# A graph and expert kernel: edge index loads moved from the sync queue to GpSimd in an earlier stage, and two matmul operands stacked as bfloat16 parts

## The reference

```python
# layer 1: label encoder and two graph attention layers
x = jnp.concatenate([features, emb[input_labels]], axis=-1)
x = x @ le_W1.T + le_b1                      # 512 -> 1024
x = layernorm(x) * ln_g + ln_b; x = relu(x)
h = x @ le_W2.T + le_b2                      # then two _gat_layer(...)
# layer 2: 8 experts, each token goes to one
hmid = relu(einsum('ecd,edf->ecf', buf, w1) + b1[:, None, :])
ybuf = einsum('ecf,efd->ecd', hmid, w2) + b2[:, None, :]
# layer 3: gated graph layer
Wh = x @ W_w + W_b; Uh = x @ U_w + U_b; Vh = x @ V_w + V_b
sigma = sigmoid((Wh * attn_l)[src] + (Wh * attn_r)[dst])
h = Uh + segment_sum(Vh[src] * sigma, dst) / (segment_sum(sigma, dst) + 1e-06)
# layer 4: dense feed-forward with a choice of one of 8 output matrices
```

## Time and profile before

| | us |
|---|---|
| three runs | 4713.58, 4710.1, 4685.79 |
| their median | 4710.1 |
| profiled execution | 4669.19 |
| its span, first to last instruction | 4667.5 |
| TensorE matmul busy in it | 3664.4 (79%) |
| VectorE, ScalarE, GpSimd busy | 2758.5, 905.6, 1101.4 |

### The profile page before, as it was taken

One profiled execution on the slowest core, in us unless ns is written; L12 is line 12 of the kernel. 1 busy time (PEld: TensorE's weight loads), 2 busy tenths in 40 slices (PEclk: granted clock), 3 DMA queues, 4 the chain that ended last, 5 costly groups with the idle time before them and its releaser, 6 DMA issues. The chain is left out here.

```text
span 4667.5 us, 61585 instructions
## 1 busy us (share of the span) xinstructions
PE 3664.4 (79%) x20551; PEld 1983.5 (42%) x20552; DVE 2758.5 (59%) x5295; ACT 905.6 (19%) x1933; POOL 1101.4 (24%) x1166
## 2 busy tenths in 40 slices
PE   0898566599996999736978668888888888868695
PEld 0455111133344434323643234444444444458585
DVE  3333999999985999840026455555555555577001
ACT  0232000000000000001210023333333333335231
POOL 0000000000000000001014366666666666600202
PEclk9999777799995999857975589999999999989798
DMA  1300000000001000003221155555555555750102
GB/s 62 95 11 17 1 1 1 1 28 19 10 10 48 10 19 12 3 9 118 87 67 50 44 160 163 168 166 162 164 161 166 166 163 161 157 131 10 54 31 71
DMA packets 215165, 347.33 MB, mean 74 GB/s; under 512 B 102139, under 2 KB 142569, under 8 KB 213313
## 3 DMA queue, kind: packets, MB, share of 16 engines
q0 software_dynamic: 79968, 260.10, 20.1%
q1 hardware_dynamic: 120518, 73.23, 5.3%
q10 hardware_dynamic: 14492, 11.60, 0.8%
HBM read 301.44 MB, written 43.93 MB: 74 GB/s over the span
## 5 line engine op out<-in xcount | busy, mean ns | idle before, releaser
L1755 POOL DMA_INDIRECT gated_G<-tab_d,ixall x880 | 889.9, 1011 | 532.4 <-DVE gated_sv L1785 261.2
L953 PE MATMUL dense_p_o<-dense_W,feat 128*32 128x512 f32 (+1 forms) x8400 | 880.7, 543 | 28.3 <-DVE dense_W L895 28.1
L895 DVE SCALAR_TENSOR_TENSOR dense_W<-dense_B,steep,cnt 128x512 f32<-128x512 f32 (+1 forms) x1400 | 849.0, 680 | 61.5 <-PE dense_p_o L953 48.9
L1837 PE MATMUL gated_p_sg<-gated_sv,gated_oh 128*128 128x512 f32 x1760 | 823.7, 612 | 0.4 <-DVE gated_sv L1785 0.4
L953 PEld LDWEIGHTS dense_p_o<-dense_W,feat 128*32 128x32 f32 x8400 | 361.9, 109 | 518.0 <-DVE dense_W L895 231.4
L1781 DVE TENSOR_TENSOR gated_tv<-gated_G,gated_p_b 128x1024 f32<-128x1024 f32 x220 | 268.7, 1221 | 441.2 <-DMA ffn_out_d<-experts_ye 262.3
L1837 PEld LDWEIGHTS gated_p_sg<-gated_sv,gated_oh 128*128 128x128 f32 x1760 | 333.9, 201 | 340.5 <-issue 334.8
L1828 PE MATMUL gated_p_b<-wr,gated_ohT 128*128 x2640 | 372.2, 296 | 49.0 <-issue 43.5
L760 PE MATMUL count_p_c<-count_R,count_L 128*128 128x500 bf16 x784 | 275.8, 490 | 161.7 <-DVE count_L L722 161.7
L1806 ACT ACTIVATE gated_sv<-gated_tv 128x1024 f32<-128x1024 f32 x220 | 232.5, 1057 | 635.8 <-DVE gated_tv L1781 522.7
L1325 POOL MEMSET route_up<- 128x128 f32 x1 | 0.2, 206 | 1495.4 <-POOLq L130 1495.4
(11 more groups left out here) (359 smaller groups left out, 4035.7 us busy)
## 6 DMA issues: line engine op xcount, KB each, us to landing
experts_ew<-in_ew SPq DMA_DIRECT2D x16, 1024.0 KB
gated_G<-tab_d,ixall POOLq DMA_INDIRECT x880
dense_B<-rise_d SPq DMA_DIRECT2D x12, 1024.0 KB
dense_Wd<-in_fWd ACTq DMA_DIRECT2D x1, 8192.0 KB
tab_d<-feat SPq DMA_DIRECT2D x50, 128.0 KB, 2.5
tab_d<-gated_in_rowg SPq DMA_DIRECT2D x25, 256.0 KB
ffn_in_d<-encode_zero POOLq DMA_DIRECT2D x1, 4096.0 KB, 16.7
xs_d<-encode_zero POOLq DMA_DIRECT2D x1, 4096.0 KB, 27.1
```

The lines of the kernel that those rows point to most:

```text
L895: o = nc.vector.scalar_tensor_tensor(out=out, in0=rise, scalar=C.steep[:, q * H + h:q * H + h + 1], in1=count, op0=ALU.max, op1=ALU.mult)
L953: m = nc.tensor.matmul(p_o[c % 2][h * MT:(h + 1) * MT, a, 0:n], feat[:, q, h, lo:lo + MT], W[t % 2][:, h, 0:n], start=(q == 0), stop=(q == ...
L1755: gp.indirect_dma_start(out=G[g % UN][:, j, :], out_offset=None, in_=C.tab3[:, :], in_offset=bass.IndirectOffsetOnAxis(ap=C.ix[:, g * ET + ...
L1837: t = nc.tensor.matmul(p_sg[k % 2][:, :], oh[k][:, j, :], sv[k % 2][:, j, :], start=(j == 0), stop=(j == ET - 1))
```

## The change

In `stage_encode` the label table becomes 96 rows of bfloat16: rows 0 to 23, 32 to 55 and 64 to 87 hold the first, second and third bfloat16 part of the f32 row, and the one-hot is repeated three times, so that one bfloat16 matmul of 96 rows adds all three. In `stage_gated_in` the bias is laid out in the same way, by GpSimd, with rows 0, 32 and 64 filled. The index loads move to GpSimd's list in `stage_experts`, 28 of them ahead of each expert's store (24 ahead of the last), and `C.dl` is made there by VectorE after its last expert. `C.ix` and `C.dl` are allocated one stage earlier.

```diff
@@ stage_encode
-        embT = sb("embT", [P, KC, NC]); b1 = sb("b1", [1, F]); lab_w = sb("lab_w", [NC, F])
+        embT = sb("embT", [P, KC, NC]); b1 = sb("b1", [1, F]); lab_w = sb("lab_w", [ST, F], BF16)
+        embS = sb("embS", [P, KC, ST]); iotaS = sb("iotaS", [P, ST])
...
             def _(v):
                 nc.vector.memset(ones1[:, :], 1.0).then_inc(s_one, 1)
+                nc.vector.memset(embS[:, :, :], 0.0).then_inc(s_stk, 1)
+                nc.vector.memset(iotaS[:, :], -1.0).then_inc(s_stk, 1)
+                v.wait_ge(s_stk, 2)
+                nc.vector.tensor_copy(iotaS[:, :].rearrange("p (s n) -> p s n", n=QP)[:, :, 0:NC],
+                                      C.iota[:, 0:NC].unsqueeze(1).broadcast_to([P, 3, NC])).then_inc(s_stk, 1)
                 ln_stats(nc, v, None, C.X, mv, st, rstd, s_st, s_var, s_std, 1e-5)
+                v.wait_ge(s_w, 16 * NW)
+                for c in range(KC):
+                    nc.vector.tensor_copy(embS[:, c, :].rearrange("p (s n) -> p s n", n=QP)[:, :, 0:NC],
+                                          embT[:, c, :].unsqueeze(1).broadcast_to([P, 3, NC])).then_inc(s_emb, 1)
+                v.wait_ge(s_hi, 1)
+                nc.vector.tensor_tensor(z[0:ST, :], p_u[0:ST, :, :].rearrange("p a f -> p (a f)"), lab_w[:, :], ALU.subtract).then_inc(s_rest, 1)
+                v.wait_ge(s_hi, 3)
+                nc.vector.tensor_tensor(z[2 * QP:ST, :], z[2 * QP:ST, :], lab_w[2 * QP:ST, :], ALU.subtract).then_inc(s_rest, 1)
+                v.wait_ge(s_lwc, 1)
...
-                nc.scalar.copy(lab_w[:, :], p_u[0:NC, :, :].rearrange("p a f -> p (a f)")).then_inc(s_lwc, 1)
+                nc.scalar.copy(lab_w[:, :], p_u[0:ST, :, :].rearrange("p a f -> p (a f)")).then_inc(s_hi, 1)
+                act.wait_ge(s_rest, 1)
+                nc.scalar.copy(lab_w[QP:2 * QP, :], z[QP:2 * QP, :]).then_inc(s_hi, 1)
+                nc.scalar.copy(lab_w[2 * QP:ST, :], z[2 * QP:ST, :]).then_inc(s_hi, 1)
+                act.wait_ge(s_rest, 2)
+                nc.scalar.copy(lab_w[2 * QP:ST, :], z[2 * QP:ST, :]).then_inc(s_lwc, 1)
@@ stage_experts, GpSimd and VectorE
+                def load_indices(g):
+                    off = gp.value_load(C.gofs[0:1, g:g + 1], min_val=0, max_val=E)
+                    gp.dma_start(C.ix[:, g * ET:(g + 1) * ET, :].rearrange("p c t -> p (c t)"),
+                                 C.edges[ds(off, EG), :].rearrange("(p c) t -> p (c t)", c=ET)).then_inc(s_ix, 16)
+
+                share = -(-NG // NE)
                 for e in range(NE):
+                    for g in range(e * share, min(NG, (e + 1) * share)):
+                        load_indices(g)
                     body(e, e % 2)
...
                 experts(v, body)
+                v.wait_ge(s_ix, 16 * NG)
+                nc.vector.tensor_tensor(C.dl[:, :].rearrange("p (g c) -> p g c", c=ET), C.ix[:, :, 1].rearrange("p (g c) -> p g c", c=ET),
+                                        C.gbase[:, 0:NG].unsqueeze(2).broadcast_to([P, NG, ET]), ALU.subtract).then_inc(s_dl, 1)
@@ stage_gated_in, SyncE, GpSimd, TensorE
                 def back(b, k):
-                    for g in range(b * share, min(NG, (b + 1) * share)):
-                        load_indices(g)
                     sp.wait_ge(s_row, b * 4 + 4)
...
                 late = 6
+                nc.gpsimd.memset(b3S[:, :], 0.0).then_inc(s_bs, 1)
                 for b in range(NB + late):
+                    if b == late - 2:
+                        gp.wait_ge(s_w, 64)
+                        gp.wait_ge(s_bs, 1)
+                        nc.gpsimd.tensor_copy(b3S[0:1, :], b3[:, :]).then_inc(s_bs, 1)
...
+                        nc.gpsimd.tensor_copy(b3S[2 * QP:2 * QP + 1, :], b3[:, :]).then_inc(s_bs, 1)
                     if b < NB:
                         gather(b)
...
+                pe.wait_ge(s_bs, 7)
...
-                        nc.tensor.matmul(p_a[:, a, 0:w], ones1[0:1, :], b3[0:1, lo:lo + w], start=False, stop=True).then_inc(s_a, 1)
+                        nc.tensor.matmul(p_a[:, a, 0:w], onesS[:, :], b3S[:, lo:lo + w], start=False, stop=True).then_inc(s_a, 1)
```

More of the change, by code:

```diff
@@ L63 @@
 SLOPE = 0.2
+QP = 32
+ST = 3 * QP
 BIG = float(2.0 ** 100)
@@ L543, in copy_x @@
                     nc.scalar.copy(xT[k][:, :], p_x[:, 0:KC * P]).then_inc(s_xTc, 1)
-                    nc.scalar.copy(ohT[k][:, :], p_x[0:NC, KC * P:KC * P + P]).then_inc(s_xTc, 1)
+                    nc.scalar.copy(ohT[k][:, :], p_x[0:ST, KC * P:KC * P + P]).then_inc(s_xTc, 1)
                 def root(b):
@@ L574, in _ @@
                 pe.wait_ge(s_one, 1)
+                pe.wait_ge(s_emb, KC)
                 for c in range(2):
                     for kc in range(KC):
-                        nc.tensor.matmul(p_u[0:NC, c, :], embT[:, kc, :], w1[:, KC + kc, c * 512:c * 512 + 512], start=(kc == 0), stop=False)
-                    nc.tensor.matmul(p_u[0:NC, c, :], ones1[0:1, 0:NC], b1[0:1, c * 512:c * 512 + 512], start=False, stop=True).then_inc(s_lw, 1)
+                        nc.tensor.matmul(p_u[0:ST, c, :], embS[:, kc, :], w1[:, KC + kc, c * 512:c * 512 + 512], start=(kc == 0), stop=False)
+                    nc.tensor.matmul(p_u[0:ST, c, :], ones1[0:1, 0:ST], b1[0:1, c * 512:c * 512 + 512], start=False, stop=True).then_inc(s_lw, 1)
                 project_attention_vectors(nc, p_h, wgr, alr, s_wa)
@@ L588, in turn_x @@
                         nc.tensor.transpose(p_x[:, c * P:c * P + P], xn[k][:, c * P:c * P + P], C.ident[:, :])
-                    nc.tensor.transpose(p_x[0:NC, KC * P:KC * P + P], oh[k][:, :], C.ident[:, :]).then_inc(s_xT, 1)
+                    nc.tensor.transpose(p_x[0:ST, KC * P:KC * P + P], oh[k][:, :], C.ident[:, :]).then_inc(s_xT, 1)
                 def hidden(b, k):
@@ L1560, in stage_gated_in @@
         s_one = sem("s_one"); s_xn = sem("s_xn"); s_t = sem("s_t"); s_tc = sem("s_tc"); s_a = sem("s_a"); s_row = sem("s_row"); s_x = sem("s_x")
-        s_rowd = [sem(f"s_rowd{k}") for k in range(2)]; s_ix = sem("s_ix"); s_dl = sem("s_dl")
+        s_rowd = [sem(f"s_rowd{k}") for k in range(2)]
         with nc.Block() as block:
@@ L1616, in _ @@
             def _(v):
-                nc.vector.memset(ones1[:, :], 1.0).then_inc(s_one, 1)
+                nc.vector.memset(onesS[:, :], 1.0).then_inc(s_one, 1)
                 def add_experts(b):
@@ L2319, in build @@
             stage_route(nc, C, A)
-        stage_experts(nc, C, A)
         with ExitStack() as second:
             sb, ps, sem = alloc(nc, second)
+            C.ix = sb("ixall", [P, NG * ET, 2], I32); C.dl = sb("dlall", [P, NG * ET])
+            stage_experts(nc, C, A)
             C.acc3 = sb("acc3", [P, NB * 2 * D])
-            C.ix = sb("ixall", [P, NG * ET, 2], I32); C.dl = sb("dlall", [P, NG * ET])
             with ExitStack() as third:
```

29 lines of the change are left out of this document (16 added, 13 removed).

## The result

| | before | after |
|---|---|---|
| median of the runs, us | 4702.91 (4 runs, 4685.79 to 4713.58) | 4578.5 (4 runs, 4575.02 to 4580.42) |
| ratio of the two, 95% interval | | 0.9738 (0.9705 to 0.9771) |
| profiled execution, us | 4669.19 | 4580.42 |
| its span; mean granted clock | 4667.5 | 4578.9; 0.884 |

What follows compares the result with a forecast made beforehand. The prediction took gated_in to be bound by SyncE's issue of small DMAs and encode by TensorE. Gated_in -90, experts +15 and encode -30 sum to -105, from 4710 to 4605 us, range 4550 to 4660.

Steps and rivals of the forecast that it cites:

- Gated_in, -90: Gated_in without index loads on SyncE: period falls to 7.3 us, stage 90 us shorter (-107 to -80).
- -78 between the rows: Gated_in, from VectorE's first row operation to its last: 253.1 us becomes 175 at a period of 7.3.
- The table: Gated_in's start: GpSimd's bias table, ready at 2414 to 2417, delays TensorE's first block by 0 to 3 us.
- Experts, +15: Experts: 220 index loads on GpSimd at 1.25 us each make the last store 15 us later.
- rival 1: Experts: GpSimd's loads overlap and are hidden, at up to 1.18 us each; 4590 us in all, chance 0.35.
- Encode, -30: Encode: bfloat16 label matmuls save 40 us, the start costs 10; net -30 (-15 to -33).
- The start: Encode's start: TensorE begins 2.2 us later, the label table adds 5.8, slower clock after idling 2; +10.
- 3: Gated_in finds another wait, TensorE at half clock, 9.2 us a block instead of 7.3; 4650 us, chance 0.11.
- 5: Encode: the label table costs what it saves, 0 instead of -30; 4635 us, chance 0.02.
- Rival 2: Experts: a GpSimd load costs 1.4 to 1.6 us, nothing overlapped; 4638 to 4682 us, chance 0.12.
- rival 4: Experts: GpSimd takes 2 us or more a load, so slower than before; 4770 us, chance 0.04.
- Rival 6: Gated_in: the stores' landing, not their issue, sets the block, so moving loads gives nothing there; 4695 us, chance 0.01.

Runs made afterwards that it cites:

- set 1: Kernel before unedited, then with the label table, stacked bias or index loads alone, on one chip: 1.0004, 0.9907, 1.0003, 0.9846 of the kernel before's 4481.28 us.
- sets 1 and 3: Set 3: changed kernel with four or seven loads a block left on SyncE, a one-part label table, or both halves together: 0.9691, 0.9819, 0.9734, 0.9668 of 4475.17 us.
- set 2: Changed kernel unedited, with fixed load offsets, with loads on SyncE in experts, or `Vh` copied by ScalarE: 0.9725, 0.9716, 0.968, 0.9703 of the kernel before's 4675.2 us.
- both halves together: Changed kernel with 56 index loads on GpSimd and 164 on SyncE in experts, and `Vh` copied by ScalarE: 4326.68 us, 0.9668 of the kernel before.

## Why the prediction was right, step by step

**Base and sum.** -105 was forecast, -124.4 measured between medians, on a base that is 7 us lower with a fourth run. The three terms were -90, +15, -30; the stages show -101, +21, -44.6. The third lies outside the bounds of its own term (-15 to -33).

**Gated_in, -90: right in its mechanism, too small by 11.** What bounded it was the issue of 220 small DMAs. The queue's step is shown by the loads alone, which give -90, and by the staircase of 0, 4, 7 and 9 loads. What was late next was to lie between VectorE's 6.6 and TensorE's 7.7, and I took 7.3 because of the half clock. It is 6.70. TensorE didn't stay at half clock once the waits had gone: the stretch's mean rose to 0.73, and VectorE decides, as the period of 6.17 with one copy on ScalarE says. That is 24 x 0.6 = 14 us. By its parts the term was -78 between the rows, -13 at the end and +1 at the start, and it is -92 (253.1 - 160.9), -11 (18.5 - 7.4) and +2. With f32 bias the period is 7.26: the bias part is worth 24 x 0.56 = 13 less its table. The table was priced at 0 to 3 us. GpSimd's chain on it is the row of 768 from 2381.67 to 2389.04, 7.4 us where I had 8, and the first row operation stands 23.3 us after the stage's start instead of 21.2, which is the 2 us assumed.

**Experts, +15: the pitch was a little high, the rest of the stage a little low.** I took 1.25 us a load out of 0.85 to 1.6 and it is 1.14. With 1.14 my own sum has the last store at 2125.5 + 251 + 9, before 2394.8, so nothing late at all. Yet it is 16 us late. What I left out is the wait of 19.65 us at the first store. I had let GpSimd issue loads without a break, though its list has only 28 of them ahead of that store and the first expert needs 53 us. With it the sum is 251 + 9 + 20 = 280, and 1.3 us ahead of the first load and some 5 us of longer gaps (three are 2.06) make the 286 measured from the stage's first DMA to the last store. So rival 1, with its limit of p = 1.18, had the right pitch and the wrong result, and the forecast got to +15 by a pitch too high and a wait that was missing: two errors that nearly cancel, so luck. The runs show the pitch to be 0.54 of DMA and 0.61 of register load, one behind the other; a list that is shorter (120 loads) or quicker (fixed offsets) is no longer late, and the stage is 274 to 275 long by the marks by which the kernel before has 269.4. The other 4 us of the 21 come behind the store, see the last section, and so does most of what is left here; 0.9 is the memset ahead of the first gather.

The price of 600 ns from the Trainium skill ("DMA: Bandwidth & Descriptors", "Latency and other measured facts") was right, but not the sum in which I put it, 0.545 + 0.60 + 0.30: the gap of 0.30 between two gathers isn't added to it.

**Encode, -30: the label matmul saves more, its start costs less.** 50 x 0.80 = 40 became 24 x 2.04 = 49 between the first copy of `feat` and the last. I had the matmul's own step (0.84 by the rows). I left out that the 24 rows, not only their type, kept TensorE from loading weights ahead, on both sides of the label matmul. The start was priced at +10. The table was 8.4 us late, against 2.2 + 5.8 = 8.0, which agrees only in sum. Its terms are +4.9, -2.3 and +5.7: TensorE starts 4.9 later, because it now waits for VectorE, whose statistics end at 127.93 instead of 125.43 and whose two small copies take 1.15; the table's matmuls are 2.3 us quicker in this pair of profiles; and the chain of copies takes 6.73 instead of 1.00, which is the term that held (5.8). The first copy of `feat` is only 4.5 late, so 4.5 - 49 = -44.5. In set 1 it is 10.8 late, and the whole is -36.8 in the profiles and -43 in the runs. So the blocks are under-priced by 7 to 9 us in both pairs, and the rest of the miss is in good part the luck of this pair of profiles.

**Rivals.** 3 (9.2 us a block in gated_in) is excluded by 6.70; 5 by encode's -44.6. Rival 2 (1.4 to 1.6 us a load) and rival 4 (2 us or more) are excluded by the pitch of 1.14. Rival 6, for which the Trainium skill's page "DMA: Bandwidth & Descriptors", section "Issuing engines are not separate DMA queues", speaks, is excluded by -101: nine loads took 9.07 + 1.0 = 10.1 us of SyncE's time a block, with DMA engines 0.20 busy, so the time to issue was the larger.

## What to carry to other kernels

A queue that is busy for a whole block with small DMAs bounds a stage though the DMA engines are idle; count its instructions and move only as many as free it: with four of nine left, gated_in was as fast as with none, and in the stage that took the others no store waited for a load, though it was 5 us longer than before (274.1 against 269.4, the open 4 us among them). An edit worth nothing alone (the bias) was worth 11 us when the bound in front of it had gone, so read what is second before dropping it. When a small matmul stands among full ones, look at the weight loads' idle times, not only at the matmul's duration: here 96 rows, zeros included, were quicker than 24. No run has a number of rows between them.

## What was not expected of the hardware

- A register load ahead of a DMA on GpSimd takes 0.61 us in which the engine does nothing else: the pitch is 1.14 us with it and 0.53 without.
- A weight load of 24 rows wasn't taken ahead of running matmuls of 128 rows (0.76 us idle before it), one of 96 rows was (0.24). The one-row bias of gated_in does the same: its f32 weight load stands 0.76 behind the last one with the loads alone moved, and that of the 96-row form 0.24 in the changed kernel. The Trainium skill, "TensorE: Matmul & The Clock Gate", section "The mechanism" of the part on packing, has a list that says that weight loads overlap with matmuls in flight only when they go to other rows of the array; the text above that list also names a spare weight buffer as a second case. The rows are against the list: 96 rows lie on those of the running 128, and their load stands beside the matmul. Why 24 rows don't, neither the page nor a run shows.
- `stage_gated`, the same in all kernels, took 1205 to 1212 us in the eight profiles of sets 1 and 3 and 1407 to 1445 in those of the result and of set 2 (one of which gathers other rows); the rest of the kernel before is 3261 us long on the first chip and 3268 in set 1. The cause stays open.
- The next stage begins 8.8 us after the last store's start in the changed kernel (2366.94 to 2375.75) and 4.8 before (2394.34 to 2399.13, set 1). The store lands after 3.4 and 3.1 us, so some 3.8 us have no row. It is 8.3 with 120 loads and 8.7 with 45 and `dl` made elsewhere in both, and 8.8 with fixed offsets, so neither the number of loads on GpSimd nor `dl` is its cause. It is 9.6 with both halves together. With all loads on SyncE it is 10.0, but there `dl` is what ends last. The cause stays open.
